# Expert results weighted by their gates in the tile and added by the indirect transfer to output rows that hold the residual

## The reference, cut to what matters

```python
def _L3_ffn_ref(x, router_w, w1, w2, w3):
    flat = x.reshape(-1, C)
    probs = jax.nn.softmax(flat @ router_w.T, axis=-1)
    topk_probs, topk_idx = jax.lax.top_k(probs, TOP_K)
    topk_probs = topk_probs / (jnp.sum(topk_probs, axis=-1, keepdims=True) + 1e-09)
    onehot = jax.nn.one_hot(topk_idx, N_EXPERTS, dtype=flat.dtype)
    gates = jnp.einsum('nk,nke->ne', topk_probs, onehot)
    h1 = jnp.einsum('nc,ehc->neh', flat, w1)
    h3 = jnp.einsum('nc,ehc->neh', flat, w3)
    y = jnp.einsum('neh,ech->nec', jax.nn.silu(h1) * h3, w2)
    return jnp.einsum('ne,nec->nc', gates, y).reshape(B, T, C)
...
t = t + _L3_ffn_ref(_ln_t(t), L3_ffn_router_w, L3_ffn_w1, L3_ffn_w2, L3_ffn_w3)
```

## Time and profile before

| what | us |
|---|---|
| median of 3 runs (lowest to highest) | 1230.27 (1229.73 to 1235.08) |
| the profiled execution, its own time | 1225.98 |
| its span, first to last instruction | 1224.1 |
| routing stage with its sends, about 618 to 844 | 226 |
| tile loop, 844 to 1184 | 340 |
| last scatters, read-back, mix and store, 1184 to 1224.1 | 40.1 |

### The profile page before, as it was taken

The page is one execution under the profiler, slowest core; times in us unless marked ns, Lnnn a source line. Parts: engine busy times, 40 slices in busy tenths (PEclk is TensorE's granted clock), DMA queues, the critical chain, the costliest instruction groups (busy, mean ns, idle before and its releaser), DMA issues.

```text
span 1224.1 us, 21611 instructions
## 1 busy us (share of the span) xinstructions
PE 957.1 (78%) x6752; PEld 575.7 (47%) x6752; DVE 814.1 (67%) x1680; ACT 697.4 (57%) x1287; POOL 645.7 (53%) x723
## 2 busy tenths in 40 slices
PE   5869999969997886678686555523999999999960
PEld 3435555534457452334353333311666666666640
DVE  7976666668848335667575444551877787787757
ACT  1815555544462557678564343212888888888850
POOL 3925555516778002003226555564677777777775
PEclk9969999979997997799898787655999999999985
DMA  5000000010023000001100000011011111111105
GB/s 202 1 2 1 1 2 1 2 65 1 1 80 104 0 1 1 1 2 29 48 7 22 20 20 20 19 44 40 26 35 31 34 33 32 35 30 36 30 24 204
DMA packets 24321, 39.37 MB, mean 32 GB/s; under 512 B 6212, under 2 KB 14168, under 8 KB 23960
## 3 DMA queue, kind: packets, MB, share of 16 engines
q1 hardware_dynamic: 15128, 28.62, 7.3%
q0 software_dynamic: 9088, 9.39, 2.4%
HBM read 24.52 MB, written 13.47 MB: 31 GB/s over the span
## 4 chain that ended last, share of the span: by engine, by line
PE 36%; POOL 18%; DVE 18%; issue 15%; ACT 8%; another core or an unknown queue 3%; SPq 1%; DMA 1%; POOLq 0%; DVEq 0%; ACTq 0%
POOL results L709 11%; POOL stage L721 7%; PE bank L1732 5%; PE bank L1743 2%; PE bank L1734 2%; PE bank L1808 2%; PE bank L1982 2%; PE bank L1757 2%; PE bank L1938 1%; PE bank L1961 1%; DVE T L807 1%; PE bank L1821 1%; PE bank L1856 1%; PE bank L1760 1%
## 5 line engine op out<-in xcount | busy, mean ns | idle before, releaser
L2175 PE MATMUL bank<-stage,big 128*114 128x512 f16 x936 | 243.2, 382 | 6.4 <-issue 3.1
L1339 DVE TENSOR_TENSOR T<-bank,T 114x512 f32<-114x512 f32 x234 | 161.5, 690 | 99.7 <-ACT T L1655 83.3
L686 POOL DMA_INDIRECT slots<-T,index x128 | 124.3, 971 | 121.0 <-DVE index L1250 84.5
L709 POOL DMA_INDIRECT results<-stage,small x156 | 153.1, 981 | 37.8 <-issue 37.8
L1655 ACT ACTIVATE T<-bank 114x512 f32<-114x512 f32 x234 | 139.7, 597 | 48.0 <-PE bank L2175 44.4
L2155 PEld LDWEIGHTS bank<-l2w,stage 114*128 114x128 f16 x1872 | 121.0, 98 | 56.2 <-issue 17.5
L1638 ACT ACTIVATE stage<-T 114x512 f16<-114x512 f32 x234 | 146.1, 625 | 0.3 <-DVE T L1339 0.3
L2155 PE MATMUL bank<-l2w,stage 114*128 x1872 | 143.6, 219 | 2.4 <-DVE stage L1349 1.4
L2175 PEld LDWEIGHTS bank<-stage,big 128*114 x936 | 107.9, 131 | 52.2 <-issue 14.6
L721 POOL TENSOR_TENSOR stage<-T,stage 114x512 f16<-114x512 f32 x78 | 89.9, 1153 | 55.7 <-ACT stage L1638 46.8
L1349 DVE TENSOR_TENSOR stage<-T,stage 114x512 f16<-114x512 f32 x156 | 106.4, 682 | 0.0
(11 more groups left out here) (386 smaller groups left out, 2007.9 us busy)
## 6 DMA issues: line engine op xcount, KB each, us to landing
stage<-slots SPq DMA_DIRECT2D x39, 130.0 KB
stage<-in_w1l SPq DMA_DIRECT2D x8, 342.0 KB
stage<-in_w3l SPq DMA_DIRECT2D x8, 342.0 KB
results<-stage,small POOLq DMA_INDIRECT x156
T<-in_xw SPq DMA_DIRECT2D x4, 512.0 KB, 6.0
X<-in_xi SPq DMA_DIRECT2D x1, 2048.0 KB, 14.6
slots<-T,index POOLq DMA_INDIRECT x128
A<-results SPq DMA_DIRECT2D x4, 512.0 KB, 6.7
```

Source lines behind the costliest of these rows:

```text
L686: pool.indirect_dma_start(slots_d, bass.IndirectOffsetOnAxis(ap=index[:, k, n:n + 1], axis=0), rows5[:, n * RW:(n + 1) * RW], None).then_i ...
L709: pool.indirect_dma_start(results_d, bass.IndirectOffsetOnAxis(ap=IDS[t % 4][:, i:i + 1], axis=0), Y5[t % 2][:, i, :], None).then_inc(S(f" ...
L1339: nc.vector.tensor_tensor(H5[q], bank[3 + q][0:HB, :], S5[q], ALU.mult).then_inc(S("hid5"), 1)
L2175: mm = nc.tensor.matmul(bank[q + 3 * (v // 2)][0:HB, :], big16[:, bass.ds(e * (4 * HID3) + (v * HID3 + k * HB), HB)], XT[s], start=(v % 2 ...
```

## The change

A row sent to `slots` grows by one f32, the gate (`GATE`; RW = 132 fp16, moved as 66 words of 32 bits). DVE computes the gates ahead of the slots and copies the first into the row (`gate5`); for the second expert POOL copies the second gate in, where it copied a destination before. Both experts of a token now have the same destination, a row of the output. SP stores the residual chunks `T4` to the output in the routing stage, as ACT makes them, and zeroes 512 extra output rows that take the results of empty slots (a fixed set of 512 in place of eight sets). In the loop POOL copies the gates out of the tile beside the destinations, DVE multiplies `Y5` by them, and the indirect DMA adds (`compute_op=ALU.add`) to the output row. Since two adds to one row must not overlap, a tile's scatters wait until those of the tile before have landed. The read-back, the mix and the final store are gone.

```diff
-RW = 2 * C + 2
+RW = 2 * C + 4
+GATE = C + 1
...
             sp.wait_ge(*when("zeros5", 3))
+            for i in range(EMPTY):
+                sp.dma_start(slots_d[E * CAP + i * SLOTS:E * CAP + (i + 1) * SLOTS, :]
+                             .rearrange("(p i) v -> p (i v)", i=SUB), empty).then_inc(S("slots_empty"), 16)
+            sp.dma_start(out_rows[2 * P * TILES:2 * P * TILES + SLOTS, :].rearrange("(p i) c -> p (i c)", i=SUB),
+                         zeros_out).then_inc(S("stored"), 16)
+            for c in range(NCH):
+                sp.wait_ge(*chunk("xtok", c))
+                sp.dma_start(out_d[0:P, c * CHUNK:(c + 1) * CHUNK], ch(T4, c)).then_inc(S("stored"), 16)
             sp.wait_ge(*when("pads5", 1))
...
-            back = results_d[0:2 * P * 2 * TILES, :].rearrange("(k p n) c -> k p n c", k=2, p=P)
-            for i in range(4):
-                ns = slice(16 * i, 16 * i + 16)
-                for k in range(2):
-                    sp.dma_start(G5[k][:, ns, :], back[k][:, ns, :]).then_inc(S(f"back_{i}"), 16)
-            for c in range(NCH):
...
-                sp.dma_start(out_d[:, c * CHUNK:(c + 1) * CHUNK], ch(T4, c)).then_inc(S("stored"), 16)
-            sp.wait_ge(*when("stored", 16 * NCH))
...
-                    nc.gpsimd.tensor_copy(dest5[:, ns], later5[:, ns]).then_inc(S("dest5_later"), 1)
-                    pool.wait_ge(*when("dest5_later", 2 * c + q + 1))
+                    nc.gpsimd.tensor_copy(gate5[:, ns], gates5[:, 1, ns]).then_inc(S("gate5_later"), 1)
+                    pool.wait_ge(*when("gate5_later", 2 * c + q + 1))
...
                 nc.gpsimd.tensor_copy(IDS[t % 4], XS[t % 2].bitcast(U32)[:, :, C]).then_inc(S("ids5"), 1)
+                nc.gpsimd.tensor_copy(GATES[t % 4], XS[t % 2].bitcast(F32)[:, :, GATE]).then_inc(S("ids5"), 1)
 
             def results5(t, subs):
-                pool.wait_ge(*when("y5", t + 1))
-                pool.wait_ge(*when("ids5", t + 1))
+                pool.wait_ge(*when("gated5", t + 1))
+                pool.wait_ge(*when("ids5", 2 * (t + 1)))
+                if t >= 1:
+                    pool.wait_ge(*when(f"resulted_{(t - 1) % 2}", 16 * SUB * ((t - 1) // 2 + 1)))
+                else:
+                    pool.wait_ge(*when("stored", 16 * (NCH + 1)))
                 for i in subs:
                     pool.indirect_dma_start(
-                        results_d, bass.IndirectOffsetOnAxis(ap=IDS[t % 4][:, i:i + 1], axis=0),
-                        Y5[t % 2][:, i, :], None).then_inc(S(f"resulted_{t % 2}"), 16)
+                        out_rows, bass.IndirectOffsetOnAxis(ap=IDS[t % 4][:, i:i + 1], axis=0),
+                        Y5[t % 2][:, i, :], None, compute_op=ALU.add).then_inc(S(f"resulted_{t % 2}"), 16)
...
+                nc.vector.tensor_copy(gate5[:, 8 * c:8 * c + 8], ga).then_inc(S4("gate5"), 1)
...
                 if within(k - 3):
+                    gates_of(k - 3)
                     index5(k - 3)
-                    gates_of(k - 3)
...
                 nc.vector.tensor_tensor(Y5[s], Y5[s], y[:, :, 1, :], ALU.add).then_inc(S("y5"), 1)
+                dve.wait_ge(*when("y5", t + 1))
+                dve.wait_ge(*when("ids5", 2 * (t + 1)))
+                nc.vector.tensor_tensor(Y5[s], Y5[s], GATES[t % 4].unsqueeze(2).broadcast_to([P, SUB, C]), ALU.mult) \
+                    .then_inc(S("gated5"), 1)
...
-            for i, c in enumerate((0, 2, 4, 6, 7)):
-                dve.wait_ge(*when(f"back_{c // 2}", 32))
...
-                nc.vector.tensor_tensor(xtokn[:, ns, :], xtokn[:, ns, :], G5[0][:, ns, :], ALU.add) \
-                    .then_inc(S("mixed5"), 1)
```

More of the change, by code:

```diff
@@ L48 @@
          "nlow1", "bq2", "bk2", "bv2", "bo2", "ga3", "be3", "n14", "bo4", "n24", "cb1",
-         "eps6", "eps5", "eps3", "tiny", "ln10", "ln20", "ln16", "guard", "one", "par0", "par1", "half0", "half1", "row0"] + [f"dump{m}" for m in range(8 * SUB)] + [f"cap{e}" for e in range(E)]
+         "eps6", "eps5", "eps3", "tiny", "ln10", "ln20", "ln16", "guard", "one", "par0", "par1", "half0", "half1", "row0"] + [f"dump{m}" for m in range(SUB)] + [f"cap{e}" for e in range(E)]
         + [f"w2c{h}" for h in range(HEADS)] + [f"b1_{e}" for e in range(E)]
@@ L446, in network @@
         WS5 = [stage[:, HID3 * i:HID3 * i + HID3] for i in range(2)]
-        zeros5 = stage[:, 4608 - 8 * SUB * (RW // 2):4608]
+        zeros5 = stage[:, 4608 - SUB * (RW // 2):4608]
+        zeros_out = stage[:, 3840:3840 + SUB * C]
+        out_rows = out_d.rearrange("q (n c) -> (q n) c", c=C)
         rows5 = T2X[:, :].bitcast(F16)
+        rows5u = T2X[:, :].bitcast(U32)
         rows5v = rows5.rearrange("p (n v) -> p n v", v=RW)
         dest5 = T2X[:, :].bitcast(U32).rearrange("p (n v) -> p n v", v=RW // 2)[:, :, C]
-        later5 = small[:, 600:664].bitcast(U32)
+        gate5 = T2X[:, :].rearrange("p (n v) -> p n v", v=RW // 2)[:, :, GATE]
         dest5f = small[:, 664:728]
@@ L468, in network @@
         IDS = [small[:, 856 + SUB * i:856 + SUB * i + SUB].bitcast(U32) for i in range(4)]
-        G5 = [t.rearrange("p (n c) -> p n c", c=C) for t in (A[:, :], X[:, :])]
-        xtokn = T4.rearrange("p (n c) -> p n c", c=C)
+        GATES = [small[:, 936 + SUB * i:936 + SUB * i + SUB] for i in range(4)]
         s16 = stage[:, :].bitcast(F16)
@@ L528, in _ @@
                 sp.dma_start(slots_d[bass.ds(row, SLOTS), :].rearrange("(p i) v -> p (i v)", i=SUB),
-                             empty[:, e, :]).then_inc(S("slots_empty"), 16)
-            sp.wait_ge(*when("slots_empty", 16 * (E + 1)))
+                             empty).then_inc(S("slots_empty"), 16)
+            sp.wait_ge(*when("slots_empty", 16 * (E + EMPTY)))
             for k in range(2):
@@ L733, in _ @@
                         ids5(t + 1)
-            for c in (1, 3, 5):
-                pool.wait_ge(*when(f"back_{c // 2}", 32))
-                ns = slice(8 * c, 8 * c + 8)
-                for k in range(2):
-                    g = G5[k][:, ns, :]
-                    nc.gpsimd.tensor_tensor(g, g, gates5[:, k, ns].unsqueeze(2).broadcast_to([P, 8, C]), ALU.mult) \
-                        .then_inc(S("mix5_pool"), 1)
-                pool.wait_ge(*when("mix5_pool", 3 * (c // 2) + 2))
-                nc.gpsimd.tensor_tensor(G5[0][:, ns, :], G5[0][:, ns, :], G5[1][:, ns, :], ALU.add) \
-                    .then_inc(S("mix5_pool"), 1)
-                pool.wait_ge(*when("mix5_pool", 3 * (c // 2) + 3))
-                nc.gpsimd.tensor_tensor(xtokn[:, ns, :], xtokn[:, ns, :], G5[0][:, ns, :], ALU.add) \
-                    .then_inc(S("mixed5_pool"), 1)
         @block.vector
@@ L2315 @@
             "half0": np.arange(128) < 64, "half1": np.arange(128) >= 64}
+    for m in range(SUB):
+        vecs[f"dump{m}"] = 2 * P * TILES + SUB * np.arange(128) + m
     for e in range(E):
         vecs[f"w2c{e}"] = w["L0_conv_cpb_w2"][e]
-        for m in range(SUB):
-            vecs[f"dump{e * SUB + m}"] = 2 * P * 2 * TILES + e * SLOTS + SUB * np.arange(128) + m
         vecs[f"cap{e}"] = np.full(128, e * CAP)
```

51 lines of the change are left out of this document (18 added, 33 removed).

## The result

The changed kernel takes 1303.53 us (median of 4 runs, 1301.89 to 1305.75) against 1230.0 for the kernel before: 1.058 times, 95% interval 1.056 to 1.060. I had forecast 1204.2 with a range of 1198 to 1230. The tail's gain is there. The loop lost three times as much.

What follows compares the result with a forecast made beforehand. PE was taken as busy 329.3 of 340 us in the loop, with POOL's two low halves links of its cycle, then a 40.1 us tail. 1230.27 with -28.3 + 0 + 1 + 0 + 1.2 = -26.1 gave 1204.2, range 1198 to 1230.

Steps and rivals of the forecast that it cites:

- The duration of the scatter: POOL's scatters in the loop: an adding one follows the number of rows and stays at 0.97 us, cost 0.
- This rival: Building adding scatters costs POOL more in the loop: +0.49 each, 1.0 a tile, 1244 us; ten in a hundred for +0.37 or more.
- slacks: POOL's spare time ahead of its two low halves in each loop tile: 0.92 and 0.28 us; anything beyond is paid in full.
- The wait in the loop: A tile's first pair of scatters waits for the tile before; nothing lost while L is under 3.65, cost 0.
- L: Landing of an adding scatter, counted from its start: between 2.15 and 4.17 us, taken as 3.1.
- the prediction's own bound of 3.65: Longest L that costs the loop nothing: spacing 2.73 plus slack 0.92; twelve in a hundred for L above it.
- The tail: After the loop: read-back, mix and store removed, -31.4, later last landing +3.1, together -28.3 us.
- Product with the gates: DVE's 0.41 us product, put ahead of block k=3's in the loop tile, ends before ACT's rounding: cost 0.
- Stores: Eight stores of 256 KB go out under the routing stage, where nothing waits for SP: cost 0.
- Copy of the gates: POOL's added 0.20 us copy in each loop tile uses 0.16 to 0.20 of the 0.28 slack: 1, between 0 and 10.
- The routing term: Before the loop: a new DVE copy of about 0.2 in six chunks costs 1.2 us, bounds 0 and 10.
- The signs that I named beforehand for being wrong altogether: In the loop: tile grows by 0.7; rivals' signs were longer scatter rows, and idle before a pair's first scatter released by landing.

Runs made afterwards that it cites:

- the kernel with the early product: Kernel before with gates in row and tile, their product ahead of block k=3's, writing scatters to two rows a token, mix on DVE alone: 1177.66 us, ratio 0.993.

## Why the prediction was wrong

**The duration of the scatter: the step that failed.** The argument went from the length of the row to the length of the instruction: 260 and 256 bytes both take about 0.96, "so the instruction follows the number of rows, and that stays". Both are transfers that write. The comparison could tell nothing of one that adds, and 0 was an end without a row behind it. The runs show +0.72 a scatter, mostly fixed, and 1.85 a tile. This rival stood in the text with +0.49, 1.0 a tile and ten in a hundred. That POOL is held, where, and with which slacks was right; the size was too small by a third and the chance far too low. By its own formula with 0.72 it gives 1.9. Its reason isn't shown: a third descriptor for each row would cost by the row, and most of the 0.72 doesn't. What POOL does in that time stays open.

The Trainium skill ("Collectives: The Full Stack", section "The bandwidth ceiling: the fold count and why AG ≠ RS ≠ AR") counts two read descriptors for an add and one for a copy. The traces show more packets too, but not in that proportion: 144 for 128 rows instead of 32, and 80 for 64 rows, with the queue's bytes unchanged (9.46 MB). Which of them are reads they don't tell. What it is worth in time only the runs told: POOL, which issues the transfer, pays, and the landing grows as well.

**The wait in the loop: the landing right, the way back missed.** I took L = 3.1; the chain of the changed kernel shows 3.15 to 3.40 in the loop, once 3.89, and 3.05 in the tail. But I let the next scatter start at the landing. It starts some 0.78 later, 0.7 of it put down to issue. By the prediction's own bound of 3.65, 3.21 + 0.78 = 3.99 costs 0.34 a tile, 12.6 us, where I wrote 0. With the longer scatters, which have eaten the slack, it cost 0.76 a tile, 29 us.

**The tail: nearly right.** Forecast -28.3; from the last low half on it is 5.5 - 28.5 = -23.0. (At L = 4.17 the same sum gives +6.4, not +6.8; the forecast doesn't use it.) Two terms were short. The last scatter starts 5.5 later against its low half instead of 2.2 (1192.3 against 1190.12), by the scatters' own length and the 0.78. And from the last landing (1298.4, an estimate with the 3.05 of the tail's other landing) to the end it is 2.4, not 0.4.

**Product with the gates: 0 was too low by 0.15 a tile on the chips with tiles of 8.39; on the others it is open.** I had DVE's product of k=3 end at 965.98, before ACT's rounding at 966.05. On the chips where the kernel with the early product ran, the kernel before starts the silu ahead of that rounding 0.87 behind DVE's add (944.88 and 944.01) instead of 1.02 (965.56 and 964.54), so the margin of 0.07 wasn't there. On a chip with tiles of 8.54 that kernel was not run. On the slower loop of the changed kernel it doesn't show.

**Stores: 0 holds. Copy of the gates, taken at 1: not measured alone.** In the changed kernel product, copy and the other rows cost little together: on one chip its mean tile is 11.11, with adding scatters and the wait alone 11.00. With writing scatters the mean tile is 0.30 over before on one chip and 0.12 on another. Product, copy, wait and the lengthened scatters share that, and I can't part them. The copy of the gates takes 0.37 there in the mean, not 0.20; the low half starts 0.14 behind its start in some tiles, as I had read it, but 0.42 in most. The routing term, +1.2, can be neither confirmed nor refuted, as above.

**The chances.** The signs that I named beforehand for being wrong altogether came in: scatters longer, idle released by the landing, tiles longer by over 0.7. What was missing was a price for an operation that no row showed; with no upper bound in the trace it deserved far more than ten in a hundred.

## What to carry to other kernels

A transfer that adds is another instruction to POOL than one that writes: when POOL's queue also holds links of the loop's cycle, price it there first, and not only in landing. A wait for a landing costs the landing and the engine's way back, together against the spacing that is there. Where the tail is to be shortened, take out of it what needs no adding transfer: the gates in the tile, with a mix on DVE alone, gave 0.7 to 1.1%.

## What the runs showed of the hardware

- An indirect transfer of 128 rows x 256 bytes holds POOL 0.98 us when it writes and 1.70 when it adds, and 1.70 too with 128 bytes; with 64 rows 0.91 and 1.55. These are means. In the loop an adding one is mostly 1.56 behind another scatter or a wait and 1.83 behind a low half. The low half alone is not the reason: the last tile has 1.56 behind one (1284.06), with DVE idle, and with all low halves on DVE there are scatters of 1.89 (942.37). The reason stays open.
- The landing of an adding one takes mostly 3.0 to 3.4 us in the loops, with single ones up to 4.5, and 3.05 in the changed kernel's tail, instead of 2.15.
- From a landing to the start of the scatter that waits for it 0.75 to 0.80 us pass on POOL, with writing scatters too (0.79 to 0.80); once in each run it is 1.46 to 1.49.
- DVE's low half, 0.68 or 0.69 long in 155 of 156 cases of the kernel before, takes 1.75 when it starts (967.77) beside POOL's (until 968.96): it ends 0.56 behind that. With all low halves on DVE it is back at 0.68 in nearly all. The Trainium skill ("SBUF — State Buffer", section "Who interferes with whom") says that a vector operation with two inputs in SBUF and a GpSimd operation that reads SBUF exclude each other, and the later one waits for the whole of the other; the trace agrees: 1.19 of waiting and 0.56 of work. In the loop of the kernel before the two hardly ever meet. They do in its tail: a DVE operation of the mix that takes 0.69 alone starts at 1201.08 beside POOL's (until 1202.17) and takes 1.64, again 0.55 past its end.
